# Routing the first half of the tokens during the attention, and the second half's scatters moved behind the first half's expert tiles

## The chip, the cores and the metric

The kernel runs on one core of a Trainium2 chip. The metric is the device time of one launch in microseconds (us). The core has five engines that run their own instruction streams and meet through semaphores: PE (matrix products and transposes), DVE (elementwise work and reductions), ACT (table functions, copies with a scale), POOL (elementwise work, masks and indirect DMAs), and SP, which here only issues DMAs.

## The reference

One transformer block on x of shape (4, 1024, 128) in float32: a modulated layer norm, causal attention with 16 heads of width 8 and rotary positions, a gated residual, a second modulated layer norm, and a mixture of experts with one shared expert and 7 routed ones, of which each token takes 2.

```
h = _layernorm(x) * (1 + ca) + sa
x = x + ga * attention(h, W_q, W_k, W_v, W_o)            # causal, 16 heads of 8
h = _layernorm(x) * (1 + cb) + sb
shared = (silu(h @ sg.T) * (h @ su.T)) @ sd.T             # inner width 352
probs = softmax(h @ wr.T + rb)                            # 7 experts
scores, idx = top_k(probs, 2); scores /= scores.sum()
out = shared + sum over the 2 experts of score * expert(h)
x = x + gb * out
```

## The kernel before

**Attention.** The 4 batches x 4 groups of 4 heads make 16 "quads", worked through one after the other in 10 steps each (`STEPS`). In a step PE makes two sets of scores, ACT takes their exponential (`probs`), POOL masks the diagonal, and PE multiplies the step before last with the values. Between these, each step has three slots in which PE writes one of three PSUM banks in turn, the ring (`ring_write`), and DVE or ACT empties it (`ring_item`). The ring carries the row maxima of the coming quads, the normalised output of the last one (kind "norm"), and in the last two quads (`n` = 14 and 15) the output projection of batches 0 to 2: a "turn" transposes 512 tokens, a "project" multiplies them with W_o, and DVE adds the result to `xs` and takes the statistics of the second layer norm. `quad_pieces` sets which slot has which piece. A ring piece is taken in order: DVE cannot pass one that stands ahead of another.

**Behind the attention.** The last batch is projected (L1710, L1766), then the 8 chunks of 512 tokens go through the second norm (`normalise` on ACT, L1001), a transpose (`turn_normalised`), the modulation (`modulate2`), the router's product (`router`, L1728) and the shared expert: `gate_up` (18 products of 512 columns in 3 pieces, on two pairs of PSUM banks), `silu` on ACT, `hidden` on DVE, `down` (12 products), `shared_sum`. The routed experts' weights are split into two float32r parts meanwhile (`first_part` on ACT, `second_part` on DVE).

**Routing.** The tokens are routed in two halves of 16 tiles of 128 (group 0 and 1): softmax (`softmax_shift`, `exp7`, `softmax_scale`), `ranks`, `weights`, then a count by PE (`counts`) and on DVE `prefix`, `starts`, `slots`, `experts`, which give each token's row in a table in DRAM sorted by expert, and each table tile's expert. POOL then writes the tokens' rows there with 32 indirect DMAs for each half (`scatter`, L782). All of this stands between the pieces of the shared expert, and the order on every engine is the order of the code. The second half's 32 scatters: 8 ahead of the expert tiles, the other 24 one by one between POOL's work for the first tiles (`ahead = 8`).

**Expert tiles.** The table has 38 tiles of 128 rows for each half. For a tile, SP loads its rows (`srow`, 4 buffers), PE transposes them (L1831), multiplies with gate and up (L1843, six products), transposes the product (L1864) and multiplies with down (L1854). ACT and DVE copy and combine between these; POOL reads weight and destination (L832, L835) and scatters the tile's results back (L844). PE works on several tiles at once: in step s the first transpose of tile s+1, gate and up of tile s, down of tile s-2, the second transpose of tile s-1. All 76 tiles run in one pass. The results of both halves are read back and added at the end (`read_results`, `combine`).

The queue that matters besides these is SP's: it issues in order, and a wait in it holds whatever stands behind.

Of the kernel before, what the change touches and what calls it, by code (L numbers as in the profile page):

```python
# [31 lines left out]
T = 128  # L32
# [112 lines left out]

def quad_pieces(n):
# [17 lines left out]
    units = {NQ - 2: range(4), NQ - 1: range(4, 2 * (B - 1))}.get(n, ())  # L164
    if units:
        order = [("turn", units[0])]
        for u in units[1:]:
            order += [("turn", u), ("project", u - 1)]
        order.append(("project", units[-1]))
        first = 3 * SLOTS if n == NQ - 2 else 2  # L170
        plan += [(first + k * (NS * SLOTS - first - 2) // len(order), kind, n, None, u)
                 for k, (kind, u) in enumerate(order)]
# [18 lines left out]
for _n, _pieces in [("first", first_pieces())] + [(n, quad_pieces(n)) for n in range(NQ)] + [("last", [(None, "norm", NQ - 1, None, 1)])]:  # L191
    RING_AT[_n] = range(len(RING_PIECES), len(RING_PIECES) + len(_pieces))
    RING_PIECES += _pieces
# [8 lines left out]
SHIFT_STEP = {RING_PIECES[x][2]: RING_PIECES[x][0] // SLOTS for x in BY_ACT["shift"] if RING_PIECES[x][0] is not None}  # L202
LAST_MAX = {n: max(x for x, e in enumerate(RING_PIECES) if e[2] == n and e[3] is not None) for n in range(NQ)}
# [3 lines left out]
def adaln_block(nc, x_d, wq_d, wk_d, wv_d, wo_d, sw_g_d, sw_u_d, sw_d_d, wr_d, rb_d, c_d, wmod_d,  # L207
# [10 lines left out]
    with ctx:  # L218
# [75 lines left out]
        w_raw = sb("w_raw", [D, 2, 2, NI], at=att)  # L294
# [8 lines left out]
        h2_hi = sb("h2_hi", [D, NT * T], F32R, at=before_y)  # L303
        before_y.close()
        y_in[0] = sb("y_first", [T, NT, D], at=moe)
        w_hi = sb("w_hi", [D, NE, 2, NI], F32R, at=moe)
        w_lo = sb("w_lo", [D, NE, 2, NI], F32R, at=moe)
        wd = sb("wd", [128, NE, len(IC), D], at=moe)
# [18 lines left out]
        beats = sb("beats", [T, GT, NE, NE], at=moe)  # L327
        sg = sb("sg", [128, 2, NI], at=moe)
# [4 lines left out]
        shared_only = ExitStack()  # L333
        sgs = sb("sgs", [128, 3, CH], at=shared_only)
        hid = sb("hid", [128, 2, len(IC), CH], at=shared_only)
        shared_only.close()

        acc = sb("acc", [T, 2, CG, D], at=moe)
        h_hi = sb("h_hi", [D, 2, T], F32R, at=moe)
        h_lo = sb("h_lo", [D, 2, T], F32R, at=moe)  # L340
        hid_s = sb("hid_s", [T, 2, NI], at=moe)
        hidT = sb("hidT", [128, 2, len(IC), T], at=moe)
        y_s = sb("y_s", [T, SB, D], at=moe)

# [73 lines left out]
        s_xn2 = sem("s_xn2")  # L418
        s_tp2 = sem("s_tp2")
# [7 lines left out]
        s_wraw = [sem(f"s_wraw{m}") for m in range(2)]  # L427
# [74 lines left out]
        def slot_steps(eng, first, last, body):  # L502

            for s in range(first, last + 1):
                body(0, s)

        def tile(i, r, lag):

            t = SU * i + (r - lag)
            if isinstance(t, int) and not 0 <= t < ST:
                return None
            return t, (r - lag) % SB, SU // SB * i + (r - lag) // SB

        FIRST_PART = (slice(0, TB), slice(TB, NT))
        TURN = (5, 6)
        GROUPED = 7
        PART = (slice(0, (B - 1) * TB), slice((B - 1) * TB, NT))
# [12 lines left out]
        def _(sp):  # L532
# [58 lines left out]
            sp.dma_start(w_raw[:, 0, 0, :], sw_g_d[0, :, :]).then_inc(s_ws_in, 16)  # L591
            sp.dma_start(w_raw[:, 0, 1, :], sw_u_d[0, :, :]).then_inc(s_ws_in, 16)
# [3 lines left out]
            def body(i, r):  # L596
# [7 lines left out]
                if isinstance(i, int) and n == NQ - 2:  # L604
                    pad0, _ = CST["pad"]
                    sp.wait_ge(s_in, 16 * 5)
                    sp.dma_start(slot_d.rearrange("(t p) c -> p t c", p=T),
                                 cst[:, pad0:pad0 + RW].unsqueeze(1).to_broadcast((T, ST, RW))).then_inc(s_pad_out, 16)
            quads(sp, body)


            def load_expert(e):
                if e == 0:
                    sp.wait_ge(s_ws_lo, 1)
                elif e >= 2:
# [1312 lines left out]
```

## Time and profile before

| what | value |
| --- | --- |
| three runs, us | 797.86, 798.30, 799.27; median 798.3 |
| profiled execution, us | 797.6; its span 795.9 |
| busy share of the span | PE 86%, DVE 72%, ACT 69%, POOL 43% |
| chain that ended last, by engine | PE 59%, DVE 18%, ACT 9%, issue 7%, DMA 3% |
| costliest group | ACT, exponentials, L973: 285.5 us, 320 of 941 ns |
| POOL, scatters of tokens, L782 | 64 of 1001 ns |
| POOL, scatters of results, L844 | 76 of 1003 ns |

The span is the time from the first to the last instruction that the profile shows; the execution's own time is 1.7 us longer. Busy time is not the same as being the bound: an engine may wait for another in one stage and hold all others up in the next. So the stages are read one by one, by the stretches of the span: attention up to 489.7 us, a transition up to 512, the shared expert with the routing up to 597, the expert tiles up to 772, and the end.

### The profile page before, as it was taken

What the parts mean: (1) busy time and instruction counts of PE and PEld (TensorE: products, weight loads), DVE (VectorE), ACT (ScalarE), POOL (GpSimd) and SP (SyncE); (2) the same over time, 40 slices, a digit from 0 to 9 for tenths busy, and PEclk for the clock granted to TensorE, in tenths of its full rate; (3) what the DMA queues carried; (4) which work ended last, traced back from release to release, by engine and by line L of the source; (5) the groups of instructions that cost most, each with busy time, mean ns of one, the idle gap of its engine ahead of it and who ended that gap; (6) DMA issues with size and microseconds to landing.
All of it is one profiled execution on the core that took longest, in us unless ns stands there. A gap on an engine that the chain in (4) does not pass through costs nothing.

```text
span 795.9 us, 18082 instructions
## 1 busy us (share of the span) xinstructions
PE 686.8 (86%) x5304; PEld 395.3 (50%) x5304; DVE 573.4 (72%) x2042; ACT 545.9 (69%) x1013; POOL 342.0 (43%) x551
## 2 busy tenths in 40 slices
PE   2986899999999999999999986678869989999970
PEld 1553123333333333333333434567659889999960
DVE  5797889999999999999999834574773323333543
ACT  2785259889989888989888788544325556666640
POOL 1367613232322322232322123235657887666652
PEclk9999569999999999999999999699999999999995
DMA  9246021111111111111110079202233322223425
GB/s 260 83 156 219 1 74 47 39 30 29 47 47 48 47 28 30 41 46 47 48 37 14 1 136 178 68 23 81 63 92 78 82 76 81 66 68 104 131 87 158
DMA packets 64760, 59.46 MB, mean 75 GB/s; under 512 B 10798, under 2 KB 52398, under 8 KB 64668
## 3 DMA queue, kind: packets, MB, share of 16 engines
q1 hardware_dynamic: 58924, 46.85, 23.3%
q0 software_dynamic: 4480, 9.64, 3.4%
q10 hardware_dynamic: 1264, 1.84, 0.7%
q8 instruction: 46, 0.75, 0.4%
q14 instruction: 46, 0.38, 0.2%
HBM read 33.57 MB, written 24.33 MB: 73 GB/s over the span
## 4 chain that ended last, share of the span: by engine, by line
PE 59%; DVE 18%; ACT 9%; issue 7%; DMA 3%; POOL 1%; SPq 1%; ACTq 1%; DVEq 0%; POOLq 0%
PE ps L1658 13%; PE ps L1602 10%; PE ps L1843 9%; PE ps L1681 7%; PE ps L1854 6%; DVE junk L1238 5%; ACT probs L973 5%; PE ps L1864 3%; PE ps L1758 2%; PE ps L1636 2%; DVE junk L1210 2%; PE ps L1750 2%; DMA routed_results_scratch<-y_s,s_dest 1%; PE ps L1831 1%; DVE rot L1193 1%
## 5 line engine op out<-in xcount | busy, mean ns | idle before, releaser
L973 ACT ACTIVATE probs<-ps 128x1024 f32<-128x1024 f32 (+1 forms) x320 | 285.5, 941 | 34.5 <-PE ps L1681 32.1
L1210 DVE CUSTOM_DVE_ANT_0 junk<-ps,tri 128x512 f32<-128x512 f32 (+3 forms) x512 | 218.5, 487 | 13.9 <-PE ps L1602 11.6
L1602 PE MATMUL ps<-ka,qa 61*128 61x256 bf16 (+3 forms) x788 | 186.7, 325 | 10.0 <-DVE rowmax L1210 3.0
L775 POOL TENSOR_SCALAR_AFFINE_SELECT probs<-probs 128x512 f32<-128x512 f32 x128 | 79.7, 634 | 191.8 <-ACT probs L973 191.8
L1658 PE MATMUL ps<-probs,v 128*32 128x512 f32 (+3 forms) x1536 | 157.7, 498 | 1.3 <-POOL probs L775 1.1
L1681 PE MATMUL ps<-qa,ka 64*128 64x512 bf16 (+3 forms) x768 | 144.6, 331 | 7.7 <-ACT probs L973 5.6
L1602 PEld LDWEIGHTS ps<-ka,qa 61*128 61x128 bf16 x788 | 53.0, 95 | 159.8 <-DVE rowmax L1210 80.4
L844 POOL DMA_INDIRECT routed_results_scratch<-y_s,s_dest x76 | 76.2, 1003 | 41.0 <-issue 35.0
L782 POOL DMA_INDIRECT slot_rows_scratch<-rows,slot x64 | 64.1, 1001 | 56.6 <-DVE slot L1393 30.1
L1243 DVE TENSOR_REDUCE leftmax<-ps 128x1 f32<-128x512 f32 x120 | 78.4, 686 | 8.5 <-PE ps L1602 8.5
L1532 DVE TENSOR_TENSOR hid_s<-sg,ps 128x352 f32<-128x352 f32 x76 | 39.6, 521 | 46.2 <-ACT sg L1087 46.0
L1854 PE MATMUL ps<-wd,hidT 128*128 (+1 forms) x456 | 64.3, 277 | 5.8 <-ACT hidT L1105 5.8
L1525 DVE TENSOR_TENSOR h_lo<-ps,h_hi 128x128 fp32r<-128x128 f32 x76 | 22.2, 291 | 59.7 <-ACT h_hi L1080 59.3
L1854 PEld LDWEIGHTS ps<-wd,hidT 128*128 128x128 f32 (+1 forms) x456 | 60.6, 192 | 7.4 <-issue 7.3
L1658 PEld LDWEIGHTS ps<-probs,v 128*32 128x32 f32 x1536 | 33.8, 108 | 54.5 <-issue 49.3
L1681 PEld LDWEIGHTS ps<-qa,ka 64*128 64x128 bf16 x768 | 42.5, 94 | 33.4 <-ACT probs L973 21.2
L1087 ACT ACTIVATE sg<-ps 128x352 f32<-128x352 f32 x76 | 35.2, 463 | 33.8 <-PE ps L1843 32.0
L1096 ACT ACTIVATE y_s<-ps,s_weight 128x128 f32<-128x128 f32 x76 | 27.9, 367 | 33.5 <-PE ps L1854 25.4
L1238 DVE CUSTOM_DVE_ANT_0 junk<-ps,above 128x256 f32<-128x256 f32 x136 | 49.3, 419 | 0.0
L749 POOL TENSOR_TENSOR mrest<-mneg,mparts 32x128 f32<-32x128 f32 x16 | 6.7, 417 | 92.7 <-ACT mparts L936 92.7
L1843 PE MATMUL ps<-w_hi,h_hi 128*128 x152 | 45.3, 380 | 1.2 <-issue 1.1
L1210 DVE DVE_READ_ACCUMULATOR2_ANT rowmax<- 128x1 f32 x512 | 42.6, 83 | 0.1
(195 smaller groups left out, 1168.4 us busy)
## 6 DMA issues: line engine op xcount, KB each, us to landing
slot_rows_scratch<-cst SPq DMA_DIRECT2D x1, 5396.0 KB, 36.1
srow<-slot_rows_scratch SPq DMA_DIRECT2D x76, 71.0 KB
k_parts_scratch<-qk_parts SPq DMA_DIRECT2D x12, 320.0 KB, 2.7
ka<-k_parts_scratch SPq DMA_DIRECT2D x32, 120.0 KB
q_parts_scratch<-qk_parts SPq DMA_DIRECT2D x12, 256.0 KB, 2.6
qa<-q_parts_scratch SPq DMA_DIRECT2D x32, 96.0 KB
ka<-k_parts_scratch SPq DMA_DIRECT2D x32, 80.0 KB
xs<-in_x SPq DMA_DIRECT2D x4, 512.0 KB, 9.4
```

Source lines behind the costliest of these rows:

```text
L775: nc.gpsimd.affine_select(out=p, in_=p, compare_op=ALU.is_ge, fill=0.0, base=0, pattern=[[0, HQ], [1, T]], channel_multiplier=-1).then_inc ...
L782: nc.gpsimd.indirect_dma_start(slot_d, bass.IndirectOffsetOnAxis(ap=slot[:, k, t:t + 1], axis=0), rows[:, t, :], None).then_inc(s_scatter[ ...
L844: nc.gpsimd.indirect_dma_start(y_d, bass.IndirectOffsetOnAxis(ap=s_dest[:, d:d + 1], axis=0), y_s[:, j, :], None).then_inc(s_y_out[j], 16)
L973: nc.scalar.activation(probs[(n * NS + s) % 4][:, 2 * h:2 * h + 2, 0:UNTIL[s] - FROM[s]], ps[:, 2 * h:2 * h + 2, FROM[s]:UNTIL[s]], ACT.Ex ...
L1210: last = V.tensor_tensor_reduce(out=junk[:, bank - 5, at:at + w], in0=ps[:, bank, at:at + w], in1=tri[:, CH - w:CH], scale=1.0, scalar=LOW ...
L1238: last = V.tensor_tensor_reduce(out=junk[:, bank - 5, cols], in0=ps[:, bank, cols], in1=above[:, h, q - CG, :], scale=1.0, scalar=LOW, op0 ...
L1243: last = V.reduce_max(leftmax[m][:, row, q - CG:q - CG + 1], ps[:, bank, :], AX.X)
L1602: last = MM(ps[:, bank, at:at + w], qa[m][g0:g0 + KS, c0 + q * T:c0 + (q + 1) * T], ka[m][g0:g0 + KS, d0 + k0:d0 + k0 + w], start=True, st ...
L1658: last = MM(ps[VW * h:VW * (h + 1), 4, q0:CH], v4[m][:, k, h, :], probs[(n * NS + s) % 4][:, h, p0:p0 + CH - q0], start=begins, stop=ends ...
L1681: last = MM(ps[:, 2 * pair + g, at:at + CH - q0], ka[m][g * HG:(g + 1) * HG, pair * KW + kb * T:pair * KW + (kb + 1) * T], qa[m][g * HG:(g ...
L1843: last = MM(ps[:, 1 + 2 * t2 + g, 0:NI], ht[:, t2, :], wt[:, bass.ds(e, 1), g, :], start=(k == 0), stop=(k == 2))
L1854: last = MM(ps[:, 6, 0:D], hidT[0:w, t2, c, :], wd[0:w, bass.ds(e, 1), c, :], start=(c == 0), stop=(c == len(IC) - 1))
```

## The change

1. Two written tables replace the rule for the projection's pieces in quads 14 and 15. Quad 15 now also carries the transposes ("rows") and router products ("router") of the first four chunks. DVE normalises chunks 0 and 1, POOL chunks 2 and 3, in quad 15; ACT does the square root for them at step 1 and the router's exponential at step 8.
2. Group 0's softmax, ranks and weights follow on DVE in quad 15, and its count is a ring piece of its own ("counts") ahead of the last "norm" piece.
3. The chunks of group 0 are transposed again behind the attention (`turn_rows`, from the finished rows), and only they go through the shared expert before the tiles. Chunks 4 to 7 are normalised there by ACT as before.
4. The tiles run in two passes of 38. Between them stands the shared expert of chunks 4 to 7. Group 1's routing runs on DVE one part per tile step of the first pass (`route_second`).
5. With `ALONG = 0` POOL issues all 32 scatters of group 1 behind the first pass's last tile.
6. The routed experts' weights are loaded in one go behind the attention, into a buffer of their own (`w_whole`), and not in turns with their split; the clearing of the table goes out in 12 parts during quads 1 to 12, and not as one DMA in quad 14. All loops over tiles are written out.

```diff
+FIRST_HALF = [(16, "turn", 0), (18, "turn", 1), (20, "project", 0), (22, "turn", 2), (24, "project", 1), (26, "turn", 3),
+              (28, "project", 2)]
+SECOND_HALF = [(0, "project", 3), (2, "turn", 4), (4, "turn", 5), (6, "project", 4), (8, "project", 5), (9, "rows", 0),
...
+               (20, "router", 3)]
...
-for _n, _pieces in [("first", first_pieces())] + [(n, quad_pieces(n)) for n in range(NQ)] + [("last", [(None, "norm", NQ - 1, None, 1)])]:
+for _n, _pieces in [("first", first_pieces())] + [(n, quad_pieces(n)) for n in range(NQ)] + [("last", [(None, "counts", NQ - 1, None, 0), (None, "norm", NQ - 1, None, 1)])]:
...
+                if n == 1:
+                    sp.wait_ge(s_in, 16 * 5)
+                if 1 <= n <= PADS:
+                    t0, t1 = ST * (n - 1) // PADS, ST * n // PADS
...
             sp.wait_ge(s_ring_free, len(BY_DVE))
+            for e in range(NE):
+                sp.dma_start(w_whole[:, e, 0, :], sw_g_d[1 + e, :, :]).then_inc(s_wraw[e], 16)
+                sp.dma_start(w_whole[:, e, 1, :], sw_u_d[1 + e, :, :]).then_inc(s_wraw[e], 16)
...
+            sp.wait_ge(s_scatter[0], 16 * TOP * GT)
+            for t in range(STG):
+                load_rows(t)
             read_results(0)
+            sp.wait_ge(s_scatter[1], 16 * TOP * GT)
+            for t in range(STG, ST):
+                load_rows(t)
...
             quads(pool, body)
+            for n in range(GC):
+                modulate_rows(n)
...
+                if g == 0 and STG - ALONG <= s < STG:
+                    scatter_second(s - STG + ALONG)
+            pool.wait_ge(s_expert, 1)
+            slot_steps(0, -2, 3, slot_step)
+            for x in range(ALONG, TOP * GT):
+                scatter_second(x)
+            pool.wait_ge(s_expert, GRP)
+            slot_steps(1, -2, 3, slot_step)
...
+                    if s == 1 and n == NQ - 1:
+                        deviation(0)
+                    if s == 8 and n == NQ - 1:
+                        exp7(0)
...
+                elif kind == "counts":
+                    incl = prefix(0, bank)
+                    end = starts(0, incl)
+                    slots(0, incl, bank)
+                    dve.sem_inc(s_ring_free, 1)
+                    experts(0, end)
...
+                elif done == ("norm", NQ - 1, None, 0):
+                    softmax_scale(0)
+                    dve.wait_ge(s_beats, 1)
+                    beaten(0, range(NE))
+                    ranks(0)
+                    weights(0)
...
             quads(pe, body)
+            ring_write(RING_AT["last"][0])
             values_product(5, 0, NS - 2)
             values_product(5, 0, NS - 1)
-            ring_write(RING_AT["last"][0])
+            ring_write(RING_AT["last"][1])
...
+            slot_steps(0, -1, 2, slot_step)
+            pe.wait_ge(s_shid, STG)
+            for n in range(GC, NC):
+                gate_up(n)
+                if n > GC:
+                    down(n - 1)
+            down(NC - 1)
+            pe.wait_ge(s_expert, GRP)
+            pe.wait_ge(s_shared, NC)
+            slot_steps(1, -1, 2, slot_step)
```

**DVE at the end of the attention.** Before, these rows stand around the last "norm" piece (`recip` and `xn`), with the statistics of batches 0 to 2 ahead of it and the last batch's sums (`xs`) behind it:

```order
L1138 SCALAR_TENSOR_TENSOR rstd<-part_a,part_b 128x24
L1148 RECIPROCAL rstd<-rstd 128x24
L1149 SCALAR_TENSOR_TENSOR nbias<-mean,rstd 128x24
L1260 RECIPROCAL recip<-ps 128x16
L1263 TENSOR_TENSOR xn<-ps,recip 128x4x32
L1283 TENSOR_TENSOR xs<-xs,ps 128x512
```

In the changed kernel (its own line numbers; `tot` to `expert` is the "counts" piece):

```order
L1316 TENSOR_SCALAR sel<-rank 128x112
L1322 TENSOR_TENSOR prob<-prob,sel 128x112
...
L1334 COPY tot<-ps 128x112
L1335 COPY scan<-ps 128x112
...
L1372 CAST slot<-slot_f 128x16
L1376 TENSOR_TENSOR passed<-cst,tend 1x266
L1378 TENSOR_REDUCE expert_f<-passed 1x38
L1379 TENSOR_SCALAR expert<-expert_f 1x38
L1252 RECIPROCAL recip<-ps 128x16
L1255 TENSOR_TENSOR xn<-ps,recip 128x4x32
L1269 TENSOR_TENSOR h_lo<-ps,h_hi 128x512 x2
```

The ranks, the weights and all of group 0's counting, 36 instructions from `tot` to `expert`, now stand ahead of the last "norm" piece.

**POOL in the expert tiles.** Before, in the tiles of the first half, a tile's results (`routed_results_scratch`) are followed by one scatter of the second half (`slot_rows_scratch`):

```order
L832 COPY s_weight<-srow 128x1
L835 ISA
L835 TENSOR_TENSOR s_dest<-srow,cst 128x1
L844 DMA routed_results_scratch<-y_s,s_dest 17920x128
L782 DMA slot_rows_scratch<-rows,slot 9728x142
```

Now, at the end of the first pass:

```order
L813 COPY s_weight<-srow 128x1
L816 ISA
L816 TENSOR_TENSOR s_dest<-srow,cst 128x1
L825 DMA routed_results_scratch<-y_s,s_dest 17920x128 x6
L787 DMA slot_rows_scratch<-rows,slot 9728x142 x32
```

The 32 scatters have moved behind the results of the first pass's last tile, and no tile's work stands between them.

## Rows read from the trace of the kernel before

**Rows 1.** Busy time by stretch: start:end, length, PE, PEld, DVE, ACT, POOL, PEclk, DMA, GB/s
```profile
463.40:489.70 26.30, 21.99 (x204) 8.86 (x204) 7.60 (x27) 22.13 (x29) 5.51 (x9) 1.00 1.11 187
489.70:512.00 22.30, 15.85 (x88) 14.15 (x88) 10.69 (x35) 17.08 (x34) 9.42 (x8) 0.77 0.62 119
512.00:597.00 85.00, 64.70 (x378) 53.39 (x378) 59.21 (x173) 30.83 (x54) 42.40 (x46) 0.94 0.20 61
597.00:657.00 60.00, 55.56 (x381) 53.15 (x382) 19.71 (x50) 33.37 (x117) 49.04 (x88) 0.94 0.30 78
```

**Rows 2.** Chain that ended last, shared expert to end: start, length, what
```profile
556.54 1.62 PE ps L1750 x6
558.16 2.68 PE ps L1758 x24
560.84 0.81 PE ps L1728 x8
...
597.05 1.23 PE ps L1843 x6
...
662.05 1.06 PE ps L1843 x6
...
735.14 0.98 PE ps L1843 x6
...
736.92 4.77 DMA srow<-slot_rows_scratch
...
766.22 1.00 PE ps L1843 x6
...
770.99 0.94 PE ps L1854 x6
773.21 2.22 DMA routed_results_scratch<-y_s,s_dest
```

**Rows 3.** Timeline, end of the attention: start, length, engine, line, operation [idle before]
```profile
478.40 1.06 PE L1627 MATMUL ps<-wo_gated,oT 128*128 128x128 f32 x8
481.19 3.77 ACT L973 ACTIVATE probs<-ps 128x1024 f32<-128x1024 f32 x4 [0.35 <-PE ps L1681]
484.98 1.28 ACT L995 ACT_TABLE_LOAD   x1
488.36 0.63 PE L1636 MATMUL ps<-eye,outT 128*128 128x128 f32 x4 [0.80 <-ACT outT L961]
489.40 0.29 DVE L1263 TENSOR_TENSOR xn<-ps,recip 128x128 f32<-128x128 f32 x1
```

**Rows 4.** Timeline of DVE, routing of the first half
```profile
509.88 0.26 DVE L1318 TENSOR_REDUCE rsum<-prob 128x16 f32<-128x112 f32 x1
514.48 0.22 DVE L1338 TENSOR_SCALAR sel<-rank 128x112 f32<-128x112 f32 x1
...
519.21 0.27 DVE L1355 COPY tot<-ps 128x112 f32<-128x112 f32 x1 [1.92 <-PE ps L1736]
523.57 0.17 DVE L1379 TENSOR_SCALAR tbase<-tbase 128x7 f32<-128x7 f32 x1
524.38 0.27 DVE L1385 TENSOR_TENSOR tot<-scan,tot 128x112 f32<-128x112 f32 x1
529.01 0.17 DVE L1400 TENSOR_SCALAR expert<-expert_f 1x38 int32<-1x38 f32 x1
```

**Rows 5.** Timeline, a POOL product and a DVE difference at once
```profile
503.10 1.19 POOL L793 TENSOR_TENSOR rows<-rows,mod_rows 128x512 f32<-128x512 f32 x1 [0.18 <-POOL rows L789]
503.23 1.61 DVE L1293 TENSOR_TENSOR h_lo<-hT,h_hi 128x512 fp32r<-128x512 f32 x1
```

**Rows 6.** Timeline of POOL, scatters one behind the other
```profile
538.97 0.96 POOL L782 DMA_INDIRECT slot_rows_scratch<-rows,slot  x1 [0.30 <-issue]
541.49 0.96 POOL L782 DMA_INDIRECT slot_rows_scratch<-rows,slot  x1 [0.30 <-issue]
```

**Rows 7.** Timeline of PE, the first transpose of the first tile
```profile
594.98 0.30 PE L1831 MATMUL ps<-eye,srow 128*128 128x128 f32 x1 [1.07 <-DVE xs L1420]
```

## What was predicted before the changed kernel had run

> **What bounds the kernel now.** I read the busy time by stretch first, then the chain that ended last, then the timelines of the four places that the change touches. The reader is to see a different limit in each stretch. In quad 15 and the end of the attention (463.4 to 489.7 us) PE is busy for 21.99 and ACT for 22.13 of 26.3 us, and DVE and POOL are nearly idle [rows 1]. The transition to 512 us is a chain across engines: PE 15.85 of 22.3 us at a granted clock of 0.77. The shared expert with the routing takes 85.0 us for 8 chunks, 10.6 us each; PE is busy for 64.7 of them, with 20 us of waits on DVE and ACT. The tiles run from the first gate product at 597.05 to the last at 766.22 us, 169.2 us for 75 intervals [rows 2]. Where POOL has only the tile's own work, 34 intervals take 735.14 - 662.05 = 73.1 us, 2.15 us each, and PE has no gap. 75 of those would be 161.3 us, so only 7.9 us are lost: while POOL also scatters (to 657 us, PE 55.56 of 60 us [rows 1]), and in one wait of 4.77 us for the table's rows at 736.92 us [rows 2]. Behind the last gate product stand 29.7 us to the end of the span (795.9).
>
> So the routing and the scatters of the second half, which the change moves, are not what the tiles mainly wait for. The sum below is made against the profiled execution's 797.6 us, which is 0.7 below the median of 798.3.
>
> **(a) The attention's last quad.** It gets four transposes (0.63 us each, by their like, L1636), four router products (0.81) and one more projection (1.06) [rows 3, 2]: 2.5 + 3.2 + 1.1 = 6.8 us of PE. ACT gets two table loads of 1.28 us and two short functions, 2.9 us, at step 1 between exponentials. The elementwise work (two chunks on DVE, two on POOL) lies beside it, on engines busy for 7.6 and 5.5 of 26.3 us. Low end: PE's 4.3 idle us take up their full length, 2.5. High end: PE's 6.8 and ACT's 2.9 both on the path, 9.7. PE and ACT are equally full here and wait for one another, so I go near PE's sum: **+6.5**.
>
> **(b) The count ahead of the last "norm" piece.** Before, from the end of step 8's exponentials (half of the row at 481.19, so 483.1) to the end of the last `xn` (489.7) takes 6.6 us [rows 3]. Now: the router's exponential, 0.3; softmax scale to `sel`, 514.70 - 509.88 = 4.8 less the 0.7 of a memset that moves ahead, 4.1; then `weights` up to about 6.0, with PE's count beside it. Then prefix and starts, 519.21 to 523.74, and slots and experts, 524.38 to 529.18 [rows 4], 9.3 us less two products of the shared expert within them (about 0.65 each), 8.1. With handovers 14.5, and 0.6 for the piece itself: 15.1 against 6.6, **+8.5**. It is on the path whole: DVE takes pieces in order, PE waits for all pieces before it turns the last batch (L1710 before), and nothing behind that can start. PE waits besides for `sel` in front of its last two value products (about 3 us), which this already holds. Ends: 7 (the weights hidden behind the count) and 10.
>
> At the same time POOL runs its eight products for `modulate_rows`, 1.19 us each, 9.5 us, right behind its last mask. In [rows 5] a DVE difference of two SBUF tensors, begun 0.13 us after such a product, takes 1.61 us; 1.19 - 0.13 of that is the product's remainder. The chain in (b) has about 17 instructions with two such inputs. Bounds: 0 (they fall between the products), and 8 (most of the chain only runs when POOL has finished). I take **+3**, nearer to the lower end, as about half of the chain's instructions have one input and POOL's products start before the chain does.
>
> The Trainium skill bears on this ("SBUF — State Buffer", section "SBUF: two separate sides"): VectorE and GpSimd share a port pair as an exclusive lock, held for a whole instruction, which a VectorE operation with two SBUF inputs needs against a GpSimd operation that reads SBUF. The row agrees with it. By that rule one such DVE instruction gets in between two POOL products, about 8 while POOL runs, and the rest comes after it, for some 5 us in place of my 3, and 822 in all.
>
> **(c) From the last `xn` to the first silu.** 22.3 us before [rows 1]. The chain is the same (turn, project, add, statistics, square root, ACT's normalisation, silu's table); two routers less stand in it, but all four chunks are normalised in one go. **-1.3**, between -3 and +2. The first half's scatters are not late: `slot` is ready 2 us ahead of the last `xn`, 32 of them at 1.26 us [rows 6] are 40.3, and the tiles start 64 us after it.
>
> **(d) The shared expert before the first tile.** 4 chunks in place of 8. Group 0's routing has left DVE, but two weight splits for each chunk have come in place of one, on ACT and on DVE, and one table change and back on ACT for the router stays. I keep 10.6 us for a chunk: 42.5 in place of 85.0, **-42.5**. Ends: 9.5 (-47) and 12 (-37).
>
> **(e) First to last gate product.** Two passes of 37 intervals at 2.15: 159.1. In the first pass DVE runs group 1's routing, one part in a step. Its own work for a tile is about 0.8 us (19.71 for some 24 tiles [rows 1]), which leaves 1.35 of 2.15; prefix and starts (1.95 each) and slots (3.2) are longer, by 0.6, 0.6 and 1.9: 3.1, say 3, between 0 (PE's tiles in flight cover it) and 9. The clock after the pause: 1. And the **change-over**, last gate product of one pass to the first of the next, goes along POOL: 5.7 until the last down product ends (766.22 to 771.93), 2.2 until its results' scatter has been issued (774.2), 32 scatters x 1.26 = 40.3, 1.3 until the last has landed (2.22 less 0.96), 2.5 for loading rows (between 2.2 and the 4.77 at 736.92), 2.1 from the first transpose to a gate product (594.98 to 597.05): 54.1 [rows 2, 6, 7]. The shared expert's second half fits into it: three pieces of 1.62 and a down of 2.68 are 7.5 us for a chunk, 30.2 for four. So PE idles for about 18 us. Together 159.1 + 3 + 1 + 54.1 = 217.2 against 169.2: **+48.0**. Ends: 44 (no routing cost, scatters at 1.2) and 58 (routing 9, scatters at 1.4, slow rows).
>
> **(f)** What follows the last gate product is unchanged, 0. The loads of weights in one go and the clearing in 12 parts have their cover: 2.5 MB of gate and up weights have 22 us until ACT first splits one, and POOL's first scatter comes quads after the last clearing. If a load were late it would show in (d), and its ends hold that.
>
> Sum: 6.5 + 8.5 + 3 - 1.3 - 42.5 + 48.0 = +22.2, so 819.8: forecast **820 us**. In short: the second half's shared expert now covers 30 of the 40 us of scatters that before were mostly covered by tiles, each pass has its own filling and draining, and the first half's routing sits on the attention's last chain instead of beside the shared expert.
>
> **Rivals.**
> - *DVE becomes the bound.* POOL's products hold the count up for the full 8 us, and the routing's parts cost 9 in the first pass. For it: [rows 5], and that every part waits for itself, instruction by instruction. Against it: DVE is busy for a third of the tiles' time (19.71 of 60 us). 820 + 5 + 6 = 831.
> - *The scatters are hidden.* Needed: 30.2 us of cover against 32 scatters, so 0.9 us for each. For it: POOL's 0.96 us without the pause of 0.30. Against it: no scatter in the trace comes sooner than 1.26 behind another. The change-over would be PE's: 5.7 + 31.7 + 2.1 = 39.5, 14.6 less: 805.
> - *The first half runs at PE's pace (the other side).* Place: the last `xn` to the first tile, 21 + 42.5 us here. PE's own work there is about 40 us, half of 15.85 + 64.7. If nothing else held it, the first half's scatters would be next (they let tiles start 45 us after `xn`): 18 less, 802. It decides for no change or faster only where (a) and (b) also stay at their low ends (9.5 in place of 18): 793.5. Against it: ACT's chain in (c) has no cover, and PE waited for 20 of 85 us before.
> - That the change doesn't do what it says: it does half. The scatters begin under the shared expert and outlast it; that is the forecast.
>
> **How the numbers follow.** Forecast 0.64, DVE bound 0.18, scatters hidden 0.10, PE's pace 0.08. All low ends together give 801, all high ends 848; not all fall one way, and about 1 in 10 is left out on each side: 804 to 838. Differences under 0.2% can't be told from none here. The last rival gives faster 0.06 and same 0.02; slower 0.92.
>
> **What would show it.** Each step: the last `xn` at about 508 (489.7 + 18); the first silu at 529; the first gate product at 571; 38 of them, then about 54 us, PE idle for the last 18 of them, with POOL scattering every 1.26 us; the last gate product near 788. It is wrong if the second pass starts as soon as the shared expert ends, if the last `xn` stays before 497, or if the first tile starts before 555.

## The result, and the profile after

The changed kernel takes 821.66 us (median of 4 runs, 821.24 to 824.0) against 798.33 us for the kernel before (4 runs): 1.0297 times as long, 95% interval 1.0275 to 1.0318. In a second comparison it took 821.84 us, 1.0272 times the kernel before (1.0246 to 1.0299). The forecast was 820. The profiled execution took 824.0 us, its span 822.2. The sum of the prediction was made against the profiled execution of the kernel before (797.6), so its +22.2 us is to be held against 824.0 - 797.6 = 26.4 us; between the medians the change is 23.3 us.

Busy time says little again. In the page of the changed kernel PE is busy for 694.1 us (686.8 before) and DVE for 584.3; the two rows to compare with before are these, where each digit stands for 20.6 us:

```profile
PE   2987899999999999999999993497989997399970
...
PEclk9997579999999999999999975799999999599995
```

There are two holes in PE's row, at slices 25 and 26 (493 to 534 us) and at slice 35 (699 to 719 us), and the granted clock is low in or behind both. The stretches of the changed kernel, to be read against [rows 1] (start:end, length, then busy us and instructions of PE, PEld, DVE, ACT, POOL, then the granted clock, DMA share and GB/s):

```profile
472.00:492.90 20.90, 18.58 (x120) 9.16 (x118) 7.14 (x20) 9.95 (x13) 4.31 (x5) 0.76 0.00 1
492.90:513.60 20.70, 7.21 (x44) 2.91 (x45) 19.27 (x60) 2.56 (x4) 13.13 (x13) 0.60 0.00 0
513.60:533.00 19.40, 9.61 (x52) 8.50 (x52) 6.93 (x23) 13.10 (x27) 14.81 (x16) 0.76 0.85 257
533.00:573.20 40.20, 33.88 (x207) 27.74 (x207) 20.78 (x35) 19.61 (x31) 17.45 (x24) 0.92 0.13 39
...
658.50:712.30 53.80, 33.75 (x202) 27.04 (x200) 11.87 (x19) 10.78 (x25) 35.24 (x40) 0.87 0.31 94
712.30:792.00 79.70, 79.41 (x578) 77.38 (x579) 35.38 (x84) 51.03 (x178) 48.51 (x106) 0.98 0.24 69
```

The reader is to see DVE busy for 19.27 of the 20.7 us in which the count stands on the path, with PE at 7.21; and the change-over of 53.8 us, in which PE works for 33.75 and POOL for 35.24.

The change-over itself, in the chain that ended last of the changed kernel (start, length, what). The counterpart of [rows 6] is 32 scatters, one every 1.26 us, the first begun at 666.78 and the last at 705.96 us. That last one stands in the chain as a DMA, since the chain goes on with its landing:

```profile
663.29 0.94 PE ps L1859 x6
...
665.51 0.96 POOL routed_results_scratch L825
...
666.78 0.96 POOL slot_rows_scratch L787
...
704.69 0.96 POOL slot_rows_scratch L787
705.96 2.31 DMA slot_rows_scratch<-rows,slot
708.28 1.77 DMA srow<-slot_rows_scratch
...
710.30 0.46 PE ps L1836
```

At its end PE has been idle for 16.51 us (18 were forecast). The row of PE in the timeline:

```profile
710.30 0.45 PE L1836 MATMUL ps<-eye,srow 128*128 128x128 f32 x1 [16.51 <-DMA srow<-slot_rows_scratch]
```

The count, in the timeline of the changed kernel (start, length, engine, line, operation, idle before). Before, prefix and starts took 4.5 us in all, without POOL's products beside them [rows 4]; here each `COPY scan<-scan` of DVE lasts until a product of POOL is over:

```profile
500.51 1.19 POOL L753 TENSOR_TENSOR rows<-rows,mod_rows 128x512 f32<-128x512 f32 x1 [0.18 <-POOL rows L749]
500.57 0.26 DVE L1335 COPY scan<-ps 128x112 f32<-128x112 f32 x1
500.86 0.86 DVE L1338 COPY scan<-scan 128x7 f32<-128x7 f32 x1
501.64 0.25 DVE L1339 TENSOR_TENSOR scan<-scan 128x105 f32<-128x105 f32 x1
501.66 1.28 POOL L749 TENSOR_TENSOR rows<-rows,mod_rows 128x512 f32<-128x512 f32 x1
501.93 1.04 DVE L1338 COPY scan<-scan 128x14 f32<-128x14 f32 x1
...
503.11 1.18 POOL L753 TENSOR_TENSOR rows<-rows,mod_rows 128x512 f32<-128x512 f32 x1 [0.18 <-POOL rows L749]
503.16 1.17 DVE L1338 COPY scan<-scan 128x28 f32<-128x28 f32 x1
```

The copy from PSUM (`scan<-ps`, 0.26 us) isn't held up beside the same product, and neither are the reduction and the reciprocal (0.25 us, at 498.45) a little earlier:

```profile
497.91 1.25 POOL L753 TENSOR_TENSOR rows<-rows,mod_rows 128x512 f32<-128x512 f32 x1 [0.18 <-POOL rows L749]
498.15 0.27 DVE L1323 TENSOR_REDUCE rsum<-prob 128x16 f32<-128x112 f32 x1
```

### The profile page after: what moved, and what is told of

Its sections match the earlier page's. It is cut to its first block, busy times and chain, and to the rows that moved or that the text cites. A ratio compares the mean times of both kernels' runs of the same rounds, so it can differ in the third digit from the quotient of the medians.

```text
span 822.2 us, 17965 instructions
## 1 busy us (share of the span) xinstructions
PE 694.1 (84%) x5320; PEld 396.8 (48%) x5320; DVE 584.3 (71%) x2050; ACT 539.6 (66%) x994; POOL 347.9 (42%) x554
## 4 chain that ended last, share of the span: by engine, by line
PE 59%; DVE 17%; ACT 9%; issue 7%; POOL 4%; DMA 2%; SPq 1%; ACTq 0%; DVEq 0%; POOLq 0%
PE ps L1690 13%; PE ps L1848 10%; PE ps L1613 10%; PE ps L1713 7%; PE ps L1859 6%; DVE junk L1217 5%; ACT probs L962 4%; POOL slot_rows_scratch L787 4%; PE ps L1869 3%; PE ps L1668 2%; DVE junk L1189 2%; PE ps L1776 1%; PE ps L1836 1%; PE ps L1586 1%; PE ps L1784 1%
## 5 line engine op out<-in xcount | busy, mean ns | idle before, releaser
L1690 PE MATMUL ps<-probs,v 128*32 128x512 f32 (+3 forms) x1536 | 161.1, 508 | 0.0
L787 POOL DMA_INDIRECT slot_rows_scratch<-rows,slot x64 | 62.4, 975 | 24.3 <-issue 19.2
L1713 PEld LDWEIGHTS ps<-qa,ka 64*128 64x128 bf16 x768 | 42.5, 94 | 32.1 <-ACT probs L962 21.8
```

What stands on the lines that cost most here:

```text
L787: nc.gpsimd.indirect_dma_start(slot_d, bass.IndirectOffsetOnAxis(ap=slot[:, k, t:t + 1], axis=0), rows[:, t, :], None).then_inc(s_scatter[ ...
L1690: last = MM(ps[VW * h:VW * (h + 1), 4, q0:CH], v4[m][:, k, h, :], probs[(n * NS + s) % 4][:, h, p0:p0 + CH - q0], start=begins, stop=ends ...
L1713: last = MM(ps[:, 2 * pair + g, at:at + CH - q0], ka[m][g * HG:(g + 1) * HG, pair * KW + kb * T:pair * KW + (kb + 1) * T], qa[m][g * HG:(g ...
```

## The experiments

The marks are: end of the attention's exponentials (the last one of quad 15; 484.96 us before, 494.86 in the first profile of the changed kernel, 493.47 in the second), last `xn`, first silu, first and last gate product, and the change-over between the two passes. The prediction counted (b) from the end of step 8's exponentials, one step earlier (483.1 before, 492.85 after), which gives the same differences to 0.2 us. The runs were made in four groups. In the first group (e1 to e4) and the last (e12) the kernel before took 830.05 and 831.06 us instead of 799, and the changed ones took 855 to 864 us. Their profiles agree with the others up to the last `xn`; what lies behind that is compared only within such a group.

**e1 and e12: POOL's eight products out of the count's way.** They go into steps 5 to 8 of quad 15, behind the products that normalise the same rows.

```diff
+                    if n == NQ - 1 and s in ROWS_AT:
+                        modulate_rows(ROWS_AT.index(s))
...
-            for n in range(GC):
-                modulate_rows(n)
```

> POOL's eight products for the finished rows are moved from behind its last mask into steps 5 to 8 of quad 15; nothing else is changed. Theory (POOL's products hold DVE's count up): the four single-input copies of `scan` fall from about 1.0 to 0.2 us each, and the rows and reached instructions from 1.2 to 0.3, together 5 to 6 us, so the last xn comes at about 508 instead of 513.5 and the time is 822 - 5.5 = 816. Rival A (these instructions are slow for a reason of their own, their input in PSUM or their number): they stay as they are, 822. Rival B (the products only move their cost into quad 15, where they hold up POOL's masks or DVE): the copies are fast, but the exponentials of step 8 end 2 to 4 us later than 492.9, 819 to 821.

> POOL's eight products in steps 5 to 8 of quad 15 and nothing else, once more, since the first run of this kernel was on the chip with the stalls. There the last xn came at 505.1 us, against 511.9 in another kernel of that call that still had the products beside the count. Theory (they hold the count up, and what follows is only shifted): last xn at 505 to 507 against 512 to 513.5, and 6 to 8 us less than the changed kernel's 821.7: 814 to 816, 1.018 to 1.021 times before. Rival (the gain is given back at the first half's scatters or in quad 15): last xn as expected but 818 to 821, or the exponentials end 2 us or more later than 493.

Measured: 1.0288 (1.0265 to 1.0310) and 1.0296 (1.0274 to 1.0317) times the kernel before, which with no run of the changed kernel in those groups says nothing on the time. The profiles decide: the last `xn` at 505.08 and 505.24 us; from the end of the exponentials 12.67 us both times, against 18.68 and 18.69 in the two profiles of the changed kernel, and 18.67 in e4, which belongs to e1's own group and has the products where the changed kernel has them. DVE of e12:

```profile
496.25 0.27 DVE L1327 SCALAR_TENSOR_TENSOR rows<-rank,cst 128x112 f32<-128x112 f32 x1
...
496.66 0.26 DVE L1336 COPY scan<-ps 128x112 f32<-128x112 f32 x1
496.96 0.17 DVE L1339 COPY scan<-scan 128x7 f32<-128x7 f32 x1
...
497.33 0.18 DVE L1339 COPY scan<-scan 128x14 f32<-128x14 f32 x1
```

The same copies take 0.17 and 0.18 instead of 0.86 and 1.04 us. Rival A falls; rival B too, since the exponentials end at 492.41 and 492.57. So POOL's products cost the count 6.0 us. What this edit alone is worth in the whole time, for which 6 to 8 us were expected, isn't shown: it was not timed outside these two groups.

**e2: the same products behind the count.** One line, `pool.wait_ge(s_expert, 1)`, ahead of the eight.

> POOL waits for the first half's expert list before its eight products; nothing else is changed. Theory: the count runs undisturbed, last xn at about 508. The products then lie beside the projection of the last batch; the first half's scatters start about 4 us later than now, at 517 to 518, and let a tile start at about 564, which is 3 us before the shared expert is done, so 816 to 818. Rival A (the count is slow for itself): last xn stays at 513.5 and POOL's delay adds 5 to 8 us, 826. Rival C (the first half's tiles wait for its scatters, not for the shared expert): first gate product stays at 573 or later, 822 to 826.

Measured: last `xn` at 505.00, which is 12.56 us behind the exponentials, as the theory had it. But 860.58 us, 1.0370 (1.0348 to 1.0392), 5.8 us more than e1 beside it: the scatters start at 515.08 instead of 503.48, and the first gate product comes at 591.12 instead of 588.96. So the count is as fast as in e1, and the first gate product comes 2.2 us later with scatters that start 11.6 us later. Both profiles have long waits between these marks (see "Open" below), so this isn't a price of the delay, and the rest of the 5.8 isn't settled either: the two profiled executions differ by 1.9 us only.

**e3: the count behind the last norm piece.** PE writes it into the bank of group 1's count; DVE does `prefix` and `starts` while PE turns the last batch, `slots` and `experts` behind the second scale.

```diff
+            ring_write(RING_AT["last"][0])
+            pe.wait_ge(s_sel, 1)
+            ring_taken(pe, COUNTED)
+            group_counts(0, GROUPED).then_inc(s_prefix, 1)
...
+            incl = prefix(0, GROUPED)
+            end = starts(0, incl)
             dve.wait_ge(s_ot, 2)
             second2(0)
...
             scale2(1)
+            slots(0, incl, GROUPED)
+            experts(0, end)
```

> The first half's count no longer stands ahead of the last norm piece: PE writes it behind that piece, DVE does prefix and starts while PE turns the last batch, and slots and experts behind the second scale. Theory (the count is on the path whole): last xn at about 500.5, 13 us earlier; the projection follows, and 3 to 5 us of the count show again between there and the first silu, 8 to 10 us stay gained: 812 to 814. Rival A (DVE's order: the count is as long in front of the last batch's sums as in front of xn): gain under 3 us, 819 to 822. Rival B (the first half's scatters, which start 5 us later than now, become what the tiles wait for): first silu 10 us earlier, but the first gate product only 3 to 5, 817 to 819.

Measured: last `xn` at 499.35, first silu at 522.70, 863.60 us or 1.0399 (1.0377 to 1.0421). The first two marks are the theory's (500.5 for the `xn`). The time is not: it is the longest of its group, 8.8 us above e1. The kernel was not timed outside that group; e7 has this edit together with e1's.

**e4 and e6: 12 scatters beside the first pass's last tiles** (`ALONG = 12`), e4 in the first group, e6 in the second beside **e5**, the changed kernel itself.

> ALONG = 12: the second half's first 12 scatters go out one per tile in the last 12 tiles of the first pass, 20 remain behind it. Theory (POOL's 32 scatters set the change-over, the shared expert covers 30 us of them): the change-over falls from 53.8 to 39.5, PE's own length (14.3 less; 12 scatters are 15.2), and the last 12 tiles of the first pass cost POOL 2.8 us each in place of 2.15, of which 3 to 7 us reach the path: 811 to 815. Rival A (something else than the scatters sets the change-over, as the table's rows or the weights' order): it stays above 50, 822 or more. Rival B (scatters beside tiles cost as much as behind them): the first pass grows by 12 us or more, 820 to 824.

> The changed kernel itself, as a control for the runs of this call. The four runs before it were made on another chip, where the kernel before takes 830 us, and where ACT and DVE stood still for 20 to 37 us beside POOL's scatters, in a wait that the profile can't name. Theory: those stalls belong to that chip, not to the change. If this call is on an undisturbed chip: 1.030 times before, marks as in the first profile (last xn 513.5, first gate product 573, change-over 54). If it is on the other one: 1.038 to 1.042, with a change-over of 74 to 76. Rival: the stalls are chance and come to any kernel on any chip; then the ratios and spans scatter by more than 1%.

> ALONG = 12 once more, beside the control. Theory (POOL's scatters set the change-over): the change-over is 13 to 14 us shorter than the control's and the first pass 3 to 7 longer, 7 to 11 us less in all. Rival B (scatters beside tiles cost as much as behind them): the first pass grows by 12 us or more, same time as the control.

Measured: e4 860.11 us, 1.0380 (1.0342 to 1.0417), in the group with the longer times (its stretches follow below); e5 821.84, 1.0272 (1.0246 to 1.0299), so this group is like the first comparison; e6 812.16, 1.0162 (1.0134 to 1.0189), 9.7 us less than e5. The first pass and the change-over, e5 first, then e6 (columns as above):

```profile
572.90:657.00 84.10, 81.04 (x581) 77.49 (x581) 45.66 (x139) 51.00 (x177) 47.77 (x102) 0.98 0.19 56
657.00:711.00 54.00, 34.04 (x203) 27.30 (x201) 12.08 (x19) 10.95 (x25) 35.28 (x40) 0.85 0.31 94
```

```profile
571.30:655.70 84.40, 81.43 (x579) 77.44 (x580) 45.63 (x139) 50.99 (x177) 52.64 (x106) 0.98 0.21 61
655.70:700.00 44.30, 34.22 (x203) 27.29 (x201) 12.14 (x19) 10.81 (x25) 30.59 (x37) 0.97 0.35 105
```

The change-over loses 9.7 us and the first pass gains 0.3, so the scatters set the change-over, and here they are nearly free beside tiles: two profiles of the changed kernel differ by more than 0.3 in the first pass (85.3 and 84.1). The time is inside the expected 7 to 11 us less, but by another split than expected (13 to 14 less in the change-over, 3 to 7 more in the pass); e8 shows why the change-over lost only 9.7.

In the first group it was otherwise. First pass and change-over of e1 (no scatter beside tiles) and of e4 (12 of them):

```profile
589.00:673.10 84.10, 81.10 (x581) 77.50 (x581) 45.63 (x139) 50.86 (x177) 47.62 (x102) 0.98 0.20 56
673.10:747.80 74.70, 35.47 (x203) 28.54 (x200) 12.11 (x20) 10.82 (x25) 35.83 (x44) 0.77 0.23 69
```

```profile
591.70:688.30 96.60, 86.70 (x580) 81.80 (x580) 45.99 (x139) 50.81 (x177) 56.92 (x112) 0.93 0.19 56
688.30:749.70 61.40, 38.16 (x203) 30.81 (x201) 11.85 (x19) 10.95 (x25) 26.36 (x35) 0.81 0.24 72
```

The change-over is 13.3 us shorter, as the theory wanted, but the first pass is 12.5 us longer, which is rival B of e4 to the letter. So "nearly free" holds for e6, e8, e9 and e10, and not where the kernel before takes 830 us.

**e7: e3 and e1 together; e8: with `ALONG = 12` as well.**

> The count behind the last norm piece, and POOL's eight products in steps 5 to 8 of quad 15. Theory: last xn at about 499.5, as where the count alone was moved; the count then runs without POOL's products beside it, the first silu comes 12 to 13 us earlier than the control's (at about 521) and the first gate product 8 to 12 us earlier: 8 to 12 us less than the control. Rival (the first half's scatters decide from then on): the first silu 12 us earlier, but the first gate product only 3 to 6, and 3 to 6 us less in all.

> Both of these edits and ALONG = 12. Theory (the terms stand in different stretches and add up): 15 to 23 us less than the control, which on an undisturbed chip is 799 to 807, so level with the kernel before or up to 1% slower. Rival (what is gained at the attention's end is lost again at the first half's scatters): 10 to 14 us less than the control.

Measured: e7 809.67 us, 1.0128 (1.0096 to 1.0160), 12.2 less than e5; last `xn` 498.26, first silu 517.70, first gate product 559.90, which are 13.9, 14.2 and 13.0 us earlier than e5's. e8 799.89 us, 1.0014 (0.9997 to 1.0031), 21.9 less than e5: 9.7 and 12.2 add up. Of the two edits in e7 neither was timed alone in this group. POOL in e8, around the end of the first pass and at the end of the scatters, and PE:

```profile
652.42 0.96 POOL L789 DMA_INDIRECT slot_rows_scratch<-rows,slot  x1 [0.30 <-issue]
653.68 0.96 POOL L827 DMA_INDIRECT routed_results_scratch<-y_s,s_dest  x1 [0.31 <-issue]
654.95 0.96 POOL L827 DMA_INDIRECT routed_results_scratch<-y_s,s_dest  x1 [0.30 <-issue]
656.22 0.96 POOL L827 DMA_INDIRECT routed_results_scratch<-y_s,s_dest  x1 [0.30 <-issue]
...
681.51 0.96 POOL L789 DMA_INDIRECT slot_rows_scratch<-rows,slot  x1 [0.30 <-issue]
```

```profile
677.04 2.92 PE L1782 MATMUL ps<-wds_gated,hid 128*128 128x128 f32 x24 [0.87 <-DVE xs L1394]
685.92 0.45 PE L1834 MATMUL ps<-eye,srow 128*128 128x128 f32 x1 [5.96 <-DMA srow<-slot_rows_scratch]
```

PE has begun with the shared expert at 650.12, but POOL is in arrears and scatters results until 657.18; so it comes 6 us too late at the other end. A scatter beside tiles isn't free for POOL (2 x 1.26 us and two short instructions against a tile's 2.15), only for PE, and probably only as long as the 4 result buffers hold; no run tested that limit.

**e9: 18 scatters, spread over steps 14 to 37. e10: the same with quad 15's pieces later.**

```diff
-        ALONG = 0
+        AT = list(range(14, 26, 2)) + list(range(26, 38))
+        ALONG = len(AT)
...
-                if g == 0 and STG - ALONG <= s < STG:
-                    scatter_second(s - STG + ALONG)
+                if g == 0 and s in AT:
+                    scatter_second(AT.index(s))
```

```diff
-(9, "rows", 0), (11, "rows", 1), (12, "router", 0), (14, "rows", 2), (15, "router", 1), (17, "rows", 3), (18, "router", 2),
+(10, "rows", 0), (12, "rows", 1), (14, "router", 0), (15, "rows", 2), (16, "router", 1), (17, "rows", 3), (19, "router", 2),
```

> As the kernel with all three edits, but 18 of the second half's scatters go out in the first pass, in every second step from 14 on and in every step from 26 on. With 12 of them in the last 12 steps POOL was still 6.0 us behind PE in the change-over (44.5 us; PE waited 5.96 us for the table's rows) and had three results' scatters in arrears. Theory (POOL has 0.6 us per tile to spare, and needs it earlier): the change-over falls to 39 to 40, the first pass stays at 84 to 85, so 5 to 6 us less than with 12: 794 to 795, 0.993 of the kernel before. Rival (18 beside tiles are too many, the results' scatters fall behind and hold PE): the first pass grows by 3 to 6 us, 798 to 801.

> The same, and in quad 15 the pieces `rows` and `router` stand 1 to 2 slots later, with the first `router` two slots behind `rows` 1 instead of one. Theory (the quad's 9 us, not 6.5, come partly from PE waiting for DVE at these pieces and from the lower clock behind it): the exponentials end 2 to 4 us earlier, at 489 to 491 instead of 492.5, and 2 to 4 us less in all than the kernel without it. Rival (PE's and ACT's added work by itself makes the 9 us): the same exponentials' end to within 0.7 us, or later, since the last router moves nearer to the softmax: no change.

Measured: e9 795.68 us, 0.9956 (0.9942 to 0.9971); e10 791.77 us, 0.9928 (0.9902 to 0.9953), both faster than the kernel before (798.60 in that group) by 0.4 and 0.7%. In e9 the first pass takes 85.0, the change-over 38.9 us:

```profile
559.10:644.10 85.00, 81.85 (x581) 77.79 (x581) 45.80 (x140) 50.99 (x177) 59.18 (x116) 0.98 0.23 67
644.10:683.00 38.90, 33.74 (x202) 27.13 (x200) 12.08 (x20) 10.95 (x25) 25.38 (x35) 0.99 0.38 110
```

That is PE's own length, which the prediction put at 39.5: no row of PE in it waits for the table's rows any more. In e10 the exponentials end at 490.08 us instead of e9's 492.49. Quad 15 in the second profile of the changed kernel, then in e6, whose quad 15 is the same, then in e10:

```profile
472.00:482.00 10.00, 8.59 (x56) 4.62 (x54) 4.50 (x12) 4.86 (x6) 3.80 (x4) 0.74 0.01 2
482.00:490.00 8.00, 8.00 (x64) 4.16 (x60) 2.76 (x8) 3.61 (x5) 0.64 (x1) 0.90 0.00 0
```

```profile
472.00:482.00 10.00, 8.59 (x76) 4.80 (x76) 6.00 (x18) 6.39 (x7) 5.32 (x6) 1.00 0.01 2
482.00:490.00 8.00, 7.18 (x61) 3.45 (x60) 2.76 (x8) 5.07 (x7) 0.64 (x1) 1.00 0.00 0
```

```profile
472.00:482.00 10.00, 10.00 (x94) 5.97 (x92) 6.29 (x18) 6.63 (x9) 9.49 (x10) 1.00 0.01 2
482.00:490.00 8.00, 7.13 (x68) 2.76 (x60) 3.45 (x16) 5.81 (x7) 5.74 (x6) 1.00 0.00 0
```

With the first router product two slots behind its rows PE doesn't stop for 1.05 us any more, as it does in every other kernel with these pieces (at 474.32 in the second profile, 475.86 in e6, 474.80 in e9). The granted clock doesn't follow from that stop: behind the same 1.05 us it was 0.74 and 0.90 in the second profile, 1.00 and 1.00 in e6, 1.00 and 0.79 in e9. By the medians e10 takes 3.9 us less than e9, but their two intervals overlap (0.9942 to 0.9971, 0.9902 to 0.9953), so the gain rests on the mark, 2.4 us in one execution of each.

**e11: without the square root in quad 15.** ACT copies the variances instead, so the router and the rows get other values than the reference's.

> The changed kernel with the square root of the first half's variances left out (ACT copies them), so its two table loads of 1.28 us and the wait behind them go. Theory (the two loads hold up DVE's normalisation and with it PE's pieces): the exponentials end 2.5 to 5 us earlier, and the time is 2.5 to 5 less than the changed kernel's, 817 to 819. Rival (the loads lie beside PE's work, which is what fills the quad): less than 1 us, 821.

Measured: 815.79 us, 1.0217 (1.0191 to 1.0242), which is 0.0055 of 799, 4.4 us, below e5's ratio; each of the two intervals is about 2 us wide to either side. So the square root with its two table loads costs time, probably more than the loads' own 2.6 us, though the intervals allow less. Where it costs it isn't shown: in the profiled execution the exponentials end at 496.71, later and not earlier, but that execution took 824.88 us where the other four took 815.6 to 816.3, and the granted clock was lower in quad 15.

```profile
472.00:482.00 10.00, 8.87 (x52) 5.33 (x50) 4.68 (x13) 4.04 (x5) 3.23 (x4) 0.65 0.01 2
482.00:490.00 8.00, 8.00 (x50) 4.11 (x48) 2.23 (x6) 3.18 (x4) 0.64 (x1) 0.71 0.00 0
```

## Why the prediction was right, point by point

All against the profiled executions, 797.6 and 824.0 us. The two rows (b) are split with e12, the others are differences of marks.

| step | forecast | measured | from |
| --- | --- | --- | --- |
| (a) last quad | +6.5 | +9.9 | last exponential 484.96 to 494.86 |
| (b) the count | +8.5 | +7.9 | exponentials to `xn`: 4.73 before, 12.67 in e12 |
| (b) POOL beside it | +3 | +6.0 | 12.67 in e12, 18.68 in the changed kernel |
| (c) `xn` to silu | -1.3 | -2.9 | 22.3 to 19.4 |
| (d) shared expert | -42.5 | -44.9 | 85.07 to 40.2 |
| (e) first to last gate | +48.0 | +49.6 | 169.17 to 218.8 |
| (f) the end | 0 | +0.5 | 29.7 to 30.25 |
| sum | +22.2 | +26.1 | 26.4 between the two executions, 26.3 between their spans |

The mechanism was the forecast's in every step: two passes with a change-over that goes along POOL, and the count in front of the last `xn`. The change-over was 53.8 us (forecast 54.1), the second pass 79.6, the first 85.3. Of the change-over each term came within 0.5 us of its forecast: 5.7 to the end of the last down product, 2.6 to the first scatter, 40.1 for the 32, 1.4 until the last has landed, 2.0 for the rows, 2.0 to the gate product. Five things are to be said on the sizes.

- (b), POOL beside it, was the term that was mis-sized most surely: 6.0 us and not 3, and so in every profile that has it. In the first profile (a) is off by more, 3.4 us, but that varies. I had taken half of the chain as not affected, since its instructions have one input. That was wrong for the four `COPY scan<-scan`, of 7 to 56 elements, which took 0.86 to 1.17 us instead of 0.17 to 0.19, 3.4 of the 6.0 us, and for the TENSOR_SCALAR `sel` (0.61 instead of 0.22 us). It was right for the reduction, the reciprocal and the copies from PSUM. In the prediction I had also worked out 5 us, and 822 in all, from the rule in the Trainium skill, and that estimate is nearer than mine. The sentence in the Trainium skill ("SBUF — State Buffer", section "SBUF: two separate sides") names VectorE operations in a two-port performance mode besides those with two SBUF inputs; I had read over that half. The trace fits it: a copy from SBUF to SBUF is held up, one from PSUM is not. It doesn't say in which mode a copy ran.
- (a) came out at 9.9 us in the first profile, just above its high end of 9.7, but at 8.5 in the second and at 7.1 in e6 (492.01), with the same quad 15. The 1.05 us for which PE stops (`router` behind `rows`) are in all three and were not in my sum. What differs is the granted clock, 0.76 from 472 to 493 us in the first profile and 1.00 from 472 to 490 in e6; why it fell in one and not in the other is open. I had also taken ACT's 2.9 us as half hidden, and e11 (4.4 us) says that the square root costs more than that, without saying where.
- (c) and (d) came out 4.0 us better together. They cover most of the 5.8 us by which (a) and the two rows (b) are worse together, so the total is closer than its terms. That is luck, and there is more of it: the sum misses the profiled executions by 4 us, while the median of 821.7 lies 1.7 from the 820 only because the first profile is an execution 2.3 us above the median.
- (e): the first pass took 5.7 us more than the second (4.3 in the second profile, 84.1 and 79.8), where 3 stood for the routing. No run separates what lengthens it. The 1 us for the clock after the pause had no row behind it, and nothing of it is seen: the second pass takes 79.6 us, 37 times 2.15.
- One reading in the prediction is wrong. The 4.77 us at 736.92 in [rows 2] are a link of the chain, not a wait of PE: PE worked on until 741.3 and then waited 0.38 us for the rows and 0.41 us more. The sum used the figure only as an upper bound for loading rows. And the 31.7 us in the rival's 39.5 stand where (e) has 30.2 for the same work; measured are 38.9.

The rivals. *DVE becomes the bound*: half of it was so, POOL's products at 6 of the 8 us, but not the routing in the first pass. *The scatters are hidden*: no; with 32, 20 and 14 of them behind the first pass the change-over is 54.0, 44.3 and 38.9 us, and only the last is PE's; e9 and e10 show that they can be hidden if they start early enough. *PE's pace*: no in the changed kernel, where the shared expert's half took 40.2 us. What it said would come next did come next once the count was moved: in e8 PE waits 2.91 us for the table's rows at 556.76 us, behind the first half's scatters.

So where did the intended gain go? Taking the routing and the second shared half out of the space ahead of the tiles gave 44.9 us. The shared half itself came back in the change-over, 30.2 us by the forecast's count, and 19.4 more of (e) beside it, most of it PE's idle 16.5 us; 23.9 came back at the attention's end, (a) and (b). With the order of four things changed (e10: the count, POOL's products, the scatters, the pieces of quad 15), the same plan is 6 to 7 us faster than the kernel before (0.7%), so what cost the time was the order and not the plan.

Open: what made the times of the first and last group about 30 us longer for the kernel before, and more for the others. In e1 ACT and DVE stand still beside POOL's scatters, in waits whose releaser the profile can't name (engine, what waited, us in total, times, longest):

```profile
ACT sgs L1018 <- remote: 37.3, 1, 37.3
...
DVE xs L1400 <- remote: 25.4, 1, 25.4
```

Such waits are in all five profiles of these groups, and neither e5 to e11 nor the first two profiles have one. It isn't the chip by its number alone: e9 to e11 and e12 were measured on the chip with the same number, with 798.60 and 831.06 us for the kernel before. More isn't known, and no profile of the kernel before was taken there.

## What to carry to other kernels

When work is split into two passes, price the change-over along the engine with the longest serial list (here POOL, 32 issues at 1.26 us), and start that list early enough that it ends with the work that covers it, slowly enough that what the engine does besides isn't in arrears at the start. Time this more than once: the same 12 scatters beside tiles took 9.7 us off in one group of runs, and in another the first pass grew by nearly as much as the change-over shrank. Look at what stands in front of the last item of an ordered queue: the count cost 8 us there, and behind it, where PE had work of its own, 13.0 of the 13.9 us that the last `xn` had gained still reached the first gate product (e7, together with e1's edit). And keep two elementwise engines from working on SBUF at once where one of them carries a chain of short dependent instructions: the copies from SBUF to SBUF and the instructions with two inputs in SBUF that met such an instruction of the other engine here had to wait until it was over.

## What the runs showed of the hardware that was not expected

- A DVE copy of 7 elements from SBUF to SBUF takes 0.86 us beside POOL's products of 1.19 to 1.28 us and 0.17 us without them; the DVE sum that follows it (`TENSOR_TENSOR scan<-scan`, 0.25 us) runs at the change from one of POOL's products to the next. A TENSOR_REDUCE (0.27 us) and a copy from PSUM (0.26 us) take the same time with and without them.
- The granted clock in the same place of the same quad differs between executions: from 472 to 482 us it was 0.74 in the second profile of the changed kernel and 1.00 in e6, both with PE's wait of 1.05 us for DVE within it. In one execution of e11 that took 9 us longer than the others of the same kernel it was 0.65, then 0.71.
- Beside tiles 12 scatters (e6) made the first pass 84.4 us long and 18 (e9) 85.0, which is inside the 84.1 and 85.3 of two profiles of the changed kernel with none. In the group with the longer times 12 of them (e4) made it 96.6 instead of 84.1.
